# Experts' up product in plain fp32, without the split into a rounded part and a rest

## What is computed

```python
routed = feat[sort_by_expert].reshape(E, C, D)          # E = 8 experts, C = 256 rows, D = 256
h = layer_norm(routed, ln_g, ln_b)
h = jax.nn.gelu(jnp.einsum('ecd,edf->ecf', h, w1) + b1[:, None, :])    # up product, F = 1024
h = jnp.einsum('ecf,efd->ecd', h, w2) + b2[:, None, :]                 # down product
out = routed + h
# out goes back to the rows' own places, and the layer's input is added
```

## Time and profile before

| what | us |
|---|---|
| median of 3 runs | 355.5 |
| the profiled execution | 355.91 |
| its span, first to last instruction | 354.1 |
| PE busy in it | 298.6 |
| DVE busy | 229.5 |
| POOL busy | 188.9 |
| ACT busy | 155.0 |

### The profile page before, as it was taken

One profiled execution on the slowest core, in us unless ns is written; L12 is line 12 of the kernel. 1 busy time (PEld: TensorE's weight loads), 2 busy tenths in 40 slices (PEclk: granted clock), 3 DMA queues, 4 the chain that ended last, 5 costly groups with the idle time before them and its releaser, 6 DMA issues.

```text
span 354.1 us, 6389 instructions
## 1 busy us (share of the span) xinstructions
PE 298.6 (84%) x2026; PEld 262.9 (74%) x2026; DVE 229.5 (65%) x802; ACT 155.0 (44%) x295; POOL 188.9 (53%) x288
## 2 busy tenths in 40 slices
PE   7998986999999999998841238998989898989891
PEld 3987965899999999998730117787877787979790
DVE  0369759799988998898318877676767676311000
ACT  1235746156556665565450034526162626353320
POOL 8402002256766566666720365767676767697711
PEclk9999999899999999999955555999999999999997
DMA  7970000850100001001110022254545454636100
GB/s 271 374 242 1 2 0 0 297 180 31 60 32 30 30 30 59 31 31 46 45 61 1 0 65 113 61 172 156 179 149 185 143 189 138 215 112 186 48 6 31
DMA packets 21340, 35.46 MB, mean 100 GB/s; under 512 B 2368, under 2 KB 14912, under 8 KB 21184
## 3 DMA queue, kind: packets, MB, share of 16 engines
q1 hardware_dynamic: 18752, 28.79, 23.0%
q0 software_dynamic: 2560, 6.31, 5.7%
HBM read 28.81 MB, written 6.29 MB: 99 GB/s over the span
## 4 chain that ended last, share of the span: by engine, by line
PE 57%; DVE 16%; DMA 12%; issue 5%; POOL 5%; SPq 2%; ACT 1%; DVEq 0%; ACTq 0%; POOLq 0%
PE bank L843 48%; DMA G<-rows_scratch,idx 8%; DMA xs<-x_dram 5%; PE bank L935 4%; DVE cmpb L707 3%; POOL G L388 2%; DVE bst L586 1%; DVE bank L740 1%; DVE Bm L573 1%; POOL out_dram L419 1%; PE bank L1031 1%; PE bank L996 1%; PE bank L888 1%; PE bank L962 1%; PE bank L923 1%
## 5 line engine op out<-in xcount | busy, mean ns | idle before, releaser
L339 POOL TENSOR_TENSOR pr<-pr,rs 128x1024 f32<-128x1024 f32 x16 | 31.6, 1977 | 55.4 <-DVE rs L653 47.4
L843 PE MATMUL bank<-w2s,hT 128*128 128x256 f32 x256 | 60.6, 386 | 0.0
L843 PE MATMUL bank<-yT,w1p 128*128 128x256 f32 x384 | 54.1, 294 | 0.0
L542 ACT ACTIVATE hT<-bank,b1s 128x256 f32<-128x256 f32 x64 | 26.8, 470 | 54.6 <-PE bank L843 53.9
L843 PE MATMUL bank<-Bm,pT 128*128 128x256 f32 (+1 forms) x384 | 48.6, 282 | 1.9 <-DVE pT L646 1.9
L843 PEld LDWEIGHTS bank<-w2s,hT 128*128 128x128 f32 x256 | 46.0, 190 | 5.7
L843 PE MATMUL bank<-Am,xnT 128*128 128x512 f32 (+1 forms) x192 | 49.8, 408 | 0.0
L843 PEld LDWEIGHTS bank<-yT,w1p 128*128 128x128 f32 x384 | 49.1, 196 | 0.4
L843 PEld LDWEIGHTS bank<-Bm,pT 128*128 128x128 f32 x384 | 46.2, 188 | 2.3 <-issue 2.0
L843 PEld LDWEIGHTS bank<-Am,xnT 128*128 128x128 f32 x192 | 35.7, 193 | 7.5
L398 POOL TENSOR_TENSOR w1p<-w1s,w1p 128x512 fp32r<-128x512 f32 x32 | 40.1, 1277 | 0.2
(11 more groups left out here) (129 smaller groups left out, 580.6 us busy)
## 6 DMA issues: line engine op xcount, KB each, us to landing
w1s<-w_dram SPq DMA_DIRECT2D x8, 1024.0 KB
w2s<-w_dram SPq DMA_DIRECT2D x8, 1024.0 KB
rows_scratch<-row SPq DMA_DIRECT2D x16, 256.0 KB, 2.0
xs<-x_dram SPq DMA_DIRECT2D x1, 2048.0 KB, 16.5
wk_s<-wk_dram SPq DMA_DIRECT2D x1, 1024.0 KB, 5.5
wv_s<-wv_dram SPq DMA_DIRECT2D x1, 1024.0 KB, 7.8
wqT_s<-wqT_dram SPq DMA_DIRECT2D x1, 1024.0 KB, 10.1
wo_s<-wo_dram SPq DMA_DIRECT2D x1, 1024.0 KB, 10.5
```

Source lines behind the costliest of these rows:

```text
L339: pool_mul = nc.gpsimd.tensor_tensor(p4, p4, rs[:, v, :].unsqueeze(1).unsqueeze(3).to_broadcast([P, KG, H, K8]), ALU.mult)
L542: nc.scalar.activation(hT[:, v, f, :], bank[1 + g % 2][:, h * CAP:(h + 1) * CAP], ACT.Gelu_apprx_tanh, bias=b1s[:, e * FC + f:e * FC + f + ...
L843: return nc.tensor.matmul(out_, l, r, start=start, stop=stop)
```

## The change

The three-pass product becomes one plain fp32 product of the loaded w1 with fp32 rows. `w1_high`, `w1_rest`, `y_rest`, the buffers `w1p` and `yF` and their semaphores go. ACT writes each half of the rows once. The load of w1 for expert `e` now waits for the up products of expert `e - 2` instead of its subtractions. The diff, cut to its core:

```diff
@@ allocation
-        yF = sb("yF", [P, CC, CAP])
-        yT = sb("yT", [P, 2, 2, CC, CAP], f32r)
+        yT = sb("yT", [P, 2, CC, CAP])
-        w1p = sb("w1p", [P, 2, 2, CC, F], f32r)
@@ SyncE
             for e in range(2, E):
                 v = e % 2
-                sp.wait_ge(e_w1l, W1_PARTS * (e - 1))
+                sp.wait_ge(e_h, FC // 2 * (e - 1))
                 sp.dma_start(w1s[:, v], ...).then_inc(e_w1[v], 16)
                 sp.wait_ge(e_o, ST * (e - 1))
                 sp.dma_start(w2s[:, v], ...).then_inc(e_w2[v], 16)
@@ GpSimd
-            def w1_rest(e, v, part):
-                ...
-            def y_rest(e, v):
-                ...
                 if 0 <= e < E:
                     token_rows(e)
-                    w1_rest(e, v, 0)
-                    w1_rest(e, v, 1)
                 if 0 <= k - 3 < E:
                     scatter(k - 3)
                 if 0 <= e < E:
                     gather(e)
-                    w1_rest(e, v, 2)
-                    w1_rest(e, v, 3)
                     bias(e)
-                    y_rest(e, v)
@@ ScalarE
-            def w1_high(e, v):
-                ...
             def rows(e, v):
                 act.wait_ge(e_gT, e + 1)
-                if e > 0:
-                    act.wait_ge(e_yl, CC * e)
                 if e >= 2:
                     act.wait_ge(e_h, FC // 2 * (e - 1))
                 for c in range(CC):
-                    for to in (yF[:, c, :], yT[:, 0, v, c, :]):
-                        nc.scalar.activation(to, bank[0][...], ...).then_inc(e_yT, 1)
+                    nc.scalar.activation(yT[:, v, c, :], bank[0][...], ...).then_inc(e_yT, 1)
@@ TensorE
                 if e > 0:
-                    pe.wait_ge(e_yT, 4 * e)
+                    pe.wait_ge(e_yT, CC * e)
...
                 if f == 0:
-                    pe.wait_ge(e_w1l, W1_PARTS * (e + 1))
+                    pe.wait_ge(e_w1[v], 16 * (e // 2 + 1))
...
                     if f == 0:
-                        pe.wait_ge(e_yl, CC * e + c + 1)
-                    last = mm3(bank[1 + g % 2][:, q * CAP:(q + 1) * CAP], lambda i: w1p[:, i, v, c, f * P:(f + 1) * P],
-                               lambda i: yT[:, i, v, c, :], c == 0, c == CC - 1)
+                        pe.wait_ge(e_yT, CC * e + c + 1)
+                    last = mm(bank[1 + g % 2][:, q * CAP:(q + 1) * CAP], w1s[:, v, c, f * P:(f + 1) * P],
+                              yT[:, v, c, :], c == 0, c == CC - 1)
```

More of the change, by code:

```diff
@@ L88, in build @@
         G = sb("G", [P, GB, ST, 2 * C])
-        yF = sb("yF", [P, CC, CAP])
-        yT = sb("yT", [P, 2, 2, CC, CAP], f32r)
+        yT = sb("yT", [P, 2, CC, CAP])
         hT = sb("hT", [P, 2, FC, CAP])
-        sb("rest_of_factors", [P, 2 * B * CC * COLS + 2 * GROUPS * C - 2 * GB * ST * C - 5 * CC * CAP - 2 * FC * CAP])
+        sb("rest_of_factors", [P, 2 * B * CC * COLS + 2 * GROUPS * C - 2 * GB * ST * C - 2 * CC * CAP - 2 * FC * CAP])
         bst = sb("bst", [P, T, 6])
@@ L172, in build @@
         e_w1 = [sem("w1_even"), sem("w1_odd")]
-        e_w1h, e_w1l = sem("w1_high"), sem("w1_rest")
         e_w2 = [sem("w2_even"), sem("w2_odd")]
         e_g = [sem(f"gathered{i}") for i in range(GB * ST)]
-        e_gT, e_yT, e_yl, e_h, e_hs = sem("rows_transposed"), sem("rowsT_copied"), sem("rowsT_rest"), sem("hidden_in_psum"), sem("hidden_made")
+        e_gT, e_yT, e_h, e_hs = sem("rows_transposed"), sem("rowsT_copied"), sem("hidden_in_psum"), sem("hidden_made")
         e_o, e_rb, e_fin = sem("expert_out"), sem("residual_bias"), sem("rows_final")
@@ L217, in build @@
         SLOTS = E + 3
-        W1_PARTS = 4
         def search_bank(k):
@@ L425, in _ @@
                 if 0 <= e < E:
-                    v = e % 2
                     token_rows(e)
-                    w1_rest(e, v, 0)
-                    w1_rest(e, v, 1)
                 if 0 <= k - 3 < E:
@@ L530, in rows @@
                 for c in range(CC):
-                    for to in (yF[:, c, :], yT[:, 0, v, c, :]):
-                        nc.scalar.activation(to, bank[0][:, c * CAP:(c + 1) * CAP], ACT.Identity,
-                                             scale=gbs[:, 0, c:c + 1], bias=gbs[:, 1, c:c + 1]).then_inc(e_yT, 1)
+                    nc.scalar.activation(yT[:, v, c, :], bank[0][:, c * CAP:(c + 1) * CAP], ACT.Identity,
+                                         scale=gbs[:, 0, c:c + 1], bias=gbs[:, 1, c:c + 1]).then_inc(e_yT, 1)
             def hidden(e, v, g):
@@ L560, in _ @@
                         hidden(e, e % 2, g)
-                if k < E:
-                    w1_high(k, k % 2)
                 if 0 <= u < E:
```

## The result

The changed kernel takes 380.4 us (median of 4 runs, 377.8 to 384.6) where the kernel before takes 355.8 on the same chip: 1.066 times as long (95% interval 1.060 to 1.073), 24.6 us more. Predicted were 363.0 us, with 368.5 as the upper end. The direction was right and the size far off. Ratios and their intervals leave out executions more than 1.5% above the fastest of their kernel: the one of 384.6 us here, and two of the four of the kernel before with only the load moved, the profiled one (378.0 us) among them.

The account below looks back on a forecast made before the run. Bound: a chain of waits over the slots, PE's matmuls up to `spread`, then the gather until the transposes. Products 5.5 - signals 1.7 + moved load 3.6 = +7.4 us on 355.91, so 363.3, median 363.0; range 358.3 to 368.5 us.

Parts of the forecast that it names:

- Price of a product: Up products on PE: a plain fp32 product takes 431 ns, against 355 ns for a product of three fp32r passes.
- Sum of the products: Slots 2 to 9: the longer plain products add 1.8 + 1.1 + 0.5 + 0.9 + 1.2 = 5.5 us.
- Gaps that hide it: Slots 3 to 6: PE's idle time hides growth in gaps 1 and 4; 0.45 us a slot is seen, 1.8 us altogether.
- Slot 2: Slot begun at half clock: plain products make `spread` 1.1 us later, gap 4 is hidden; cost 1.1 us.
- Relief of the signals: Slots 3 to 6: with w2 alone loading at the slot's start, PE's signals come earlier; gain 1.7 us, ends 0 and 2.1.
- the subtractions ahead of them: POOL's 32 subtractions of w1, 40.1 us busy: beside slot 7's 0.4 us, they delay nothing on the chain.
- The moved load: Slots 2 to 7: w1's load beside the gather costs 0.6 us each, 3.6 us; ends 0 and 8.4, or 1.4 a slot.
- Rival B: Slots 2 to 7: the gather is held until w1's load is through, 367.7 us; chance 0.18 together with another rival.
- The clock: TensorE: full clock except in the search alone and the very end; slot 2 begins at half clock, products there twice 431 ns.

## Why the prediction was off, step by step

The 24.4 us between the spans of the two profiled executions divide like this: 14.5 for the held gathers, 4.7 for the half clock behind three of them, and 1.2 because the search happens to begin later (187.3 instead of 186.1 us, in a part that the change leaves alone). That leaves 4.0 for the rest, which is products and signals above all, where the forecast had 5.5 less 1.7.

- **Price of a product, 431 instead of 355 ns:** right; gelu's distance is the forecast 1.72 us.
- **Sum of the products, 5.5 us:** right. The early-scatter version of the kernel before and the changed kernel with the load behind the first gather both have early scatters and free gathers; they stand at 0.992 and 1.008, 1.6% or 5.7 us apart, uncertain by some 2 us.
- **Gaps that hide it:** right in the main. From one first gather to the next, slots 3 to 6 take 17.53, 17.52, 17.71 and 17.37 us with the load behind the first gather, and 17.12, 17.12, 17.34 and 17.04 in the early-scatter version of the kernel before: 0.3 to 0.4 us a slot seen where I had 0.45. Slot 2 cost more than the forecast 1.1: from its first `total` to its first gather it takes 9.7 us instead of 8.2.
- **Relief of the signals, 1.7 us:** about the right size (0.8% or 2.9 us, 1.6 to 4.2 by the interval), for the wrong reason. I put it down to the load in the earlier trace rows. It was the place of the scatters: the subtractions ahead of them, whose removal I had called without effect, put them beside `tokens`. The trace of the kernel before spoke against the load already, in slot 7, where both loads run and Rx follows `spread` after 0.31 us.
- **The moved load, 3.6 us with 8.4 as the end:** the step that failed. "The gather's descriptors come first" holds for the first gather only. The second starts 1.28 us behind the first, at the very moment of the load. That "the load needs two microseconds to fill the engines" was no shelter either: its data begins to move 1.3 us after its issue and an undisturbed gather's 1.7 us after POOL's start. And the upper end of 1.4 us a slot was built too short: 4.4 us for the load and half a microsecond for the rest of the gather. In the trace the load takes 5.2 us to land, and the second transposes come 0.5 us behind that. Measured: 2.4 us a slot on average. The Trainium skill, "DMA: Bandwidth & Descriptors", section "Queues, rings and completion order", has the queues take turns packet by packet, and its packet is a run of typically 9 to 17 descriptors, which is drained whole before the engine changes queues. I had left that size out. The trace has 272 entries for the load on 16 DMA engines, 17 on each, and 144 or 9 on each for half of it. If such a share is one packet of the page, the whole load passes before the gather's next turn, and the trace agrees (7.0 us instead of 4.7, and 6.0 behind half of it). If a single entry of the trace were the packet, it wouldn't, with 200 entries of the load to none of the second gather's data. No run here shows the packets themselves.
- **Rival B** named the mechanism with the right sign, at 367.7 us.
- **The clock:** missed. The earlier trace rows showed half clock where PE has little to do, and I used it for slot 2 alone. A bound on a wait of PE has to include what the wait does to the clock behind it. The unused matmuls put that at about 5.7 us, the two traces at 4.7.

## What to carry to other kernels

A load that "has a slot to spare" is free only if the transfer beside which it starts has the time too: when a wait is replaced by a later one, look up what other queues issue within a microsecond or two of the new moment, count from each issue to the first data and not only to the issue, and put bulk behind the latency-bound transfer that is issued last. When a bound on a wait of TensorE is worked out, add the half-clock stretch behind it. And before splits and roundings are removed from helper engines, compare the passes by the distance of signals: here three fp32r passes (355 ns) were cheaper than one fp32 product (431 ns), and the helper work had cost nothing but the place in which it put the scatters (1.7 us in the trace).

## What the runs showed of the hardware that I had not expected

- An indirect gather of 128 rows that starts on POOL in the same moment as a 1 MB load on SyncE's queue lands after it: 5.73 us from the second gather's start to the transposes, where 3.4 is usual. Behind half the load it is held by 1.2 us. Begun 2.2 us ahead of the load it isn't held, and its data is through then before the load's begins to move. A first gather begun 0.4 us ahead, in the kernel before with only the load moved, is held as well: in slot 4 the first transposes come 6.2 us behind it, where 3.6 is usual.
- TensorE fell to half clock behind waits of 2.4 to 2.9 us, in some slots and not in others with a wait of the same length; 22 small matmuls in the wait kept the full clock.
- In slots with a search, ACT and DVE got PE's signals late (ACT stood 1.20 us in the earlier trace rows) while POOL's scatters were issued beside `tokens`, and on time with the scatters some 2.5 us earlier. In slot 7, without a search, Rx was on time beside a scatter.
